# Expert tiles by a transposing DMA: rows scattered as 16-bit planes to a region per expert, in a transformer block with linear attention and a mixture of experts

## The reference, cut to what matters

```python
x = x + attn(layernorm(x))
xf = layernorm(x)                                     # 2048 x 512
scores = xf @ gate_w.T + gate_b + bias                # 2048 x 8
top_scores, top_idx = top_k(scores, 2)
gates = softmax(top_scores)
comb = sum(one_hot(top_idx, 8) * gates[..., None], 1)
h = silu(einsum('td,ehd->teh', xf, w1) + b1)          # hidden size 352
y = einsum('teh,edh->ted', h, w2) + b2
x = x + einsum('ted,te->td', y, comb)
```

## Time and profile before

| | |
|---|---|
| median of three runs | 1009.66 us (1009.46 to 1010.25) |
| the profiled execution | span 1008.9 us from first to last instruction; its own time outside the span is not listed |
| PE busy | 995.8 us, 99% of the span |
| DVE, ACT, POOL busy | 688.1, 513.2, 255.7 us (68%, 51%, 25%) |
| DMA moved | 75.35 MB, mean 75 GB/s |

### The profile page before, as it was taken

One profiled execution on the slowest core, in us unless ns is written; L12 is line 12 of the kernel. 1 busy time (PEld: TensorE's weight loads), 2 busy tenths in 40 slices (PEclk: granted clock), 3 DMA queues, 4 the chain that ended last, 5 costly groups with the idle time before them and its releaser, 6 DMA issues.

```text
span 1008.9 us, 17463 instructions
## 1 busy us (share of the span) xinstructions
PE 995.8 (99%) x5019; PEld 839.2 (83%) x5020; DVE 688.1 (68%) x1554; ACT 513.2 (51%) x1322; POOL 255.7 (25%) x413
## 2 busy tenths in 40 slices
PE   8999999999999999999999999999999989999998
PEld 7888888888888888888788888888888879989996
DVE  6888655665666677767878778887888764544544
ACT  5444444444444447755556555555554954343442
POOL 1000000000000002222433232333333555555554
PEclk9999999999999999999999999999999999999999
DMA  7002501000000012343211121111125645555653
GB/s 263 13 30 84 209 22 40 23 21 21 21 22 21 21 63 63 105 172 116 44 44 51 42 52 42 42 42 42 42 66 149 203 123 102 107 102 101 107 108 48
DMA packets 46862, 75.35 MB, mean 75 GB/s; under 512 B 6090, under 2 KB 18555, under 8 KB 46691
## 3 DMA queue, kind: packets, MB, share of 16 engines
q1 hardware_dynamic: 37010, 56.04, 18.3%
q0 software_dynamic: 9808, 18.79, 10.2%
HBM read 53.14 MB, written 23.50 MB: 76 GB/s over the span
## 4 chain that ended last, share of the span: by engine, by line
PE 93%; DVE 3%; ACT 1%; DMA 1%; issue 1%; SPq 0%; POOL 0%; POOLq 0%; DVEq 0%; ACTq 0%
PE pK L1627 16%; PE pK L1629 16%; PE pK L1628 16%; PE pA L1627 6%; PE pA L1629 6%; PE pA L1628 6%; PE pX L1627 6%; PE pX L1629 5%; PE pX L1628 5%; PE pA L1761 3%; PE pT L1970 2%; PE pT L1707 2%; PE pX L1988 1%; PE pA L1895 1%; PE pK L1895 1%; DMA xn<-in_attn_hidden_states 1%
## 5 line engine op out<-in xcount | busy, mean ns | idle before, releaser
L973 ACT ACTIVATE qs<-q,nrec 128x64 f32<-128x64 f32 x512 | 129.6, 336 | 88.1 <-DVE nrec L1357 85.7
L594 POOL TENSOR_TENSOR wv_lo<-wv_in,wv_hi 128x512 fp32r<-128x512 f32 x4 | 5.2, 1296 | 403.5 <-ACT wo_hi L894 403.5
L1627 PE MATMUL pA<-k_hi,xn_hi 128*128 128x512 f32 x256 | 100.9, 394 | 0.6 <-DVE k_lo L1232 0.6
L1627 PE MATMUL pK<-wk_hi,xnT_hi 128*128 128x512 f32 (+1 forms) x256 | 100.1, 391 | 0.4 <-DVE wk_lo L1212 0.3
L1627 PE MATMUL pK<-wq_hi,xnT_hi 128*128 128x512 f32 x256 | 100.4, 392 | 0.0
L1629 PE MATMUL pK<-wq_hi,xnT_lo 128*128 128x512 f32 x256 | 99.9, 390 | 0.0
L1629 PE MATMUL pA<-k_hi,xn_lo 128*128 128x512 f32 x256 | 99.8, 390 | 0.0
L1628 PE MATMUL pK<-wk_lo,xnT_hi 128*128 128x512 f32 (+1 forms) x256 | 99.7, 390 | 0.0
L1628 PE MATMUL pA<-k_lo,xn_hi 128*128 128x512 f32 x256 | 99.7, 389 | 0.0
L1629 PE MATMUL pK<-wk_hi,xnT_lo 128*128 128x512 f32 (+1 forms) x256 | 99.7, 389 | 0.0
L1628 PE MATMUL pK<-wq_lo,xnT_hi 128*128 128x512 f32 x256 | 99.7, 389 | 0.0
(11 more groups left out here) (291 smaller groups left out, 2446.8 us busy)
## 6 DMA issues: line engine op xcount, KB each, us to landing
w_in<-in_ffn_w SPq DMA_DIRECT2D x22, 256.0 KB, 4.2
w_in<-in_ffn_w SPq DMA_DIRECT2D x8, 704.0 KB, 5.8
xn<-in_attn_hidden_states SPq DMA_DIRECT2D x16, 256.0 KB, 6.2
wv_in<-in_attn_Wv SPq DMA_DIRECT2D x16, 256.0 KB, 2.8
wo_in<-in_attn_Wo SPq DMA_DIRECT2D x16, 256.0 KB, 3.0
wk_in<-in_attn_Wq SPq DMA_DIRECT2D x4, 1024.0 KB, 5.7
xnT_dram<-xnT SPq DMA_DIRECT2D x4, 1024.0 KB, 11.5
x_in<-in_attn_hidden_states SPq DMA_DIRECT2D x16, 256.0 KB, 2.7
```

Source lines behind the costliest of these rows:

```text
L973: i = nc.scalar.activation(qs[:, s], q[:, s], ACT.Copy, scale=nrec[:, b * HC + h:b * HC + h + 1])
L1627: nc.tensor.matmul(dst, lhs[0], rhs[0], start=start, stop=False)
```

## The change

The normalized rows no longer go to DRAM in token order. POOL splits each tile of `xn2` into two planes of 16-bit halves (`put_planes`, a copy of 128 x 1024 uint16), and scatters the 2 KB rows twice by slot (`put_rows`), to `xr_dram`, which is laid out as `meta_dram` is: 17 x 128 rows per expert. An expert tile is then 128 consecutive rows of `xr_dram`; SP loads it with one transposing DMA (128 rows x 1024 halves) into `xgT`, two buffers, at a row number it reads from `meta_row`. ACT joins the low halves into `gx` (`act_rec`), DVE the high halves (`dve_rec`); `gT_hi` and `gT_lo` are then made from `gx` in SBUF. The four PE transposes of each tile and POOL's gathers are gone. Since unused slots must hold numbers, all of `xr_dram` (8 x 2176 rows and 128 more, of 2 KB) is zeroed in the first stage, by DMAs from a 1 KB row of zeros that is repeated. To make room, `gprod` has one buffer instead of two (each dot product waits for the one before), `hT` moves to PSUM, and tiles 0 and 1 have no second set of buffers. The scatters of the last two tiles stand around the gather of the meta rows.

```diff
 [SP]
-            for c in range(1, NC):
-                sp.wait_ge(wk_lo_ready, c * FB)
-                load_wk(c)
+            def zero_rows(first, last):
+                for e in range(first, last):
+                    sp.dma_start(xr_dram[e * EROWS * P:(e + 1) * EROWS * P, :].rearrange("(p r) (h n) -> p (r h) n", p=P, h=2),
+                                 zero16[:, :].unsqueeze(1).to_broadcast([P, 2 * EROWS, D])).then_inc(xr_zeroed, 16)
+
+            sp.wait_ge(wk_lo_ready, FB)
+            load_wk(1)
+            sp.wait_ge(zero_early, 1)
+            zero_rows(0, 3)
+            sp.wait_ge(wk_lo_ready, 2 * FB)
+            load_wk(2)
+            zero_rows(3, 6)
+            sp.dma_start(xr_dram[E * EROWS * P:MROWS * P, :].rearrange("p (h n) -> p h n", h=2),
+                         zero16[:, :].unsqueeze(1).to_broadcast([P, 2, D])).then_inc(xr_zeroed, 16)
+            sp.wait_ge(wk_lo_ready, 3 * FB)
+            load_wk(3)
...
+            zero_rows(6, E)
+            sp.wait_ge(xr_zeroed, 16 * (E + 1))
...
-                sp.wait_ge(xn2_ready, t)
-                sp.dma_start(xn2_dram[ds((t - 1) * P, P), :], xn2[:, :]).then_inc(xn2_stored, 16)
...
+            def load_tile(i):
+                if i >= 2:
+                    sp.wait_ge(rec_lo, i - 1)
+                    sp.wait_ge(rec_hi, i - 1)
+                row = sp.value_load(meta_row[i:i + 1, 0:1], min_val=0, max_val=MROWS - 1)
+                sp.dma_start_transpose(xgT[i % 2][:, :].rearrange("p (c n) -> p c n", n=P),
+                                       xr_dram[ds(row * P, P), :]).then_inc(s_xt[i % 2], 16)
+
+            sp.wait_ge(experts_ready, 1)
+            sp.wait_ge(s_xr, 32 * (NT - 1))
+            sp.wait_ge(s_xr_last, 32)
+            for i in range(NS):
+                load_tile(i)
 [POOL]
+            def put_rows(r, b):
+                rows = xp_last if isinstance(r, int) and r == NT - 1 else xp
+                pool.wait_ge(xp_ready, r + 1)
+                pool.nop(nofuse=True)
+                for c in range(2):
+                    pool.indirect_dma_start(xr_dram, bass.IndirectOffsetOnAxis(slot_i[b][:, c:c + 1].bitcast(U32), 0),
+                                            rows[:, :], None).then_inc(s_xr_last if rows is xp_last else s_xr, 16)
...
+            def put_planes(t):
+                last = isinstance(t, int) and t == NT - 1
+                pool.wait_ge(xn2_ready, t + 1)
+                if not (isinstance(t, int) and t == 0 or last):
+                    pool.wait_ge(s_xr, 32 * t)
...
+                pool.tensor_copy(planes(xp_last if last else xp), words(xn2)).then_inc(xp_ready, 1)
...
             with pool.Fori(2, NT // 2) as h:
                 for b in range(2):
+                    put_planes(2 * h + (b - 2))
                     put_mask(2 * h + (b - 2), b, 32 * h - 32)
                     put_xb(2 * h + b)
                     put_slots(2 * h + (b - 2), b)
...
-            def gather(i):
...
+            put_rows(NT - 2, 0)
             for b in range(2):
                 pool.wait_ge(s_meta[b], 16 * NT)
             pool.indirect_dma_start(meta_in[:, :], None, meta_rows, bass.IndirectOffsetOnAxis(meta_row[:, :].bitcast(U32), 0)
                                     ).then_inc(s_metain, 16)
+            put_rows(NT - 1, 1)
 [ACT]
+            def act_rec(i, b):
+                act.wait_ge(s_xt[b], 16 * (i // 2) + 16 if isinstance(i, int) else 8 * i + (16 - 8 * b))
...
+                    act.wait_ge(gT_lo_ready, i)
+                nc.scalar.copy(words(gx)[:, 0, :], planes(xgT[b])[:, 0, :]).then_inc(rec_lo, 1)
...
-                nc.scalar.copy(g_of(i)[0][:, :], g_bank(i)).then_inc(gT_hi_ready, 1)
+                nc.scalar.copy(gT_hi[:, :], gx[:, :]).then_inc(gT_hi_ready, 1)
 [DVE]
-                        dve.wait_ge(dots_done, E * t + (e - 1 - E))
+                        dve.wait_ge(dots_done, E * t + (e - E))
...
+            def dve_rec(i, b):
...
+                    dve.wait_ge(gT_lo_ready, i)
+                v.tensor_copy(words(gx)[:, 1, :], planes(xgT[b])[:, 1, :]).then_inc(rec_hi, 1)
...
             with dve.Fori(2, NS // 2) as h:
                 for b in range(2):
+                    dve_rec(2 * h + (b + 1), 1 - b)
                     dve_gT(2 * h + (b + 1))
                     dve_y(2 * h + (b - 2), b, 16 * h - 16)
                     dve_hT(2 * h + b, b)
 [PE]
                     i = 2 * h + b
                     pe_h(i, expert(i))
-                    pe_gT(2 * h + (b + 1), 1 - b)
                     pe_y(2 * h + (b - 2), b, expert(2 * h + (b - 2)))
                     pe_hT(i)
```

More of the change, by code:

```diff
@@ L29 @@
 I32 = mybir.dt.int32
+U16 = mybir.dt.uint16
 U32 = mybir.dt.uint32
@@ L215, in block_kernel @@
     gT_lo = sb("gT_lo", D, 186 * KB, F32R)
[L216 to L222, removed]
+    gx = sb("gx", D, 188 * KB)
+    h_in = sb("h_in", H, 190 * KB)
+    hT_hi = [sb("hT_hi0", HB * P, 190 * KB + 1408, F32R), sb("hT_hi1", HB * P, M0 + 5120, F32R)]
+    hT_lo = [sb("hT_lo0", HB * P, 190 * KB + 2944, F32R), sb("hT_lo1", HB * P, 190 * KB + 4480, F32R)]
+    xgT = [sb(f"xgT{b}", 2 * D, (196 + 2 * b) * KB, U16) for b in range(2)]
     y_last = sb("y_last", D, 198 * KB)
@@ L353, in block_kernel @@
         hT_ones = sem("hT_ones")
-        s_g = [sem(f"s_g{i}") for i in range(2)]
+        s_xt = [sem(f"s_xt{i}") for i in range(2)]
+        rec_lo = sem("rec_lo")
+        rec_hi = sem("rec_hi")
         s_add = [sem(f"s_add{i}") for i in range(2)]
-        gT_put = sem("gT_put")
         gT_hi_ready = sem("gT_hi_ready")
@@ L403, in block_kernel @@
         y_bank = lambda i: pA[:, (i - (NS - 2)) * 512:(i - (NS - 3)) * 512] if isinstance(i, int) and i >= NS - 2 else pK[:, 512:1024]
[L406 to L410, removed]
+        hT = pT[:, 0:HB * P]
+        planes = lambda a: a[:, :].rearrange("p (h n) -> p h n", h=2)
+        words = lambda a: a[:, :].bitcast(U16).rearrange("p (n h) -> p h n", h=2)
         @block.sync
@@ L1963, in _ @@
                     meta_transpose()
-            def pe_gT(i, b):
-                pe.wait_ge(s_g[b], 16 * (i // 2) + 16 if isinstance(i, int) else 8 * i + (16 - 8 * b))
-                if not (isinstance(i, int) and i < 2):
-                    pe.wait_ge(gT_lo_ready, i)
-                for n in range(FB):
-                    last = nc.tensor.transpose(g_bank(i)[:, n * P:(n + 1) * P], xg[:, b * D + n * P:b * D + (n + 1) * P], ident[:, :])
-                last.then_inc(gT_put, 1)
             def pe_h(i, e):
                 pe.wait_ge(gT_lo_ready, i + 1)
-                if not (isinstance(i, int) and i < 2):
+                if not (isinstance(i, int) and i < 1):
                     pe.wait_ge(h_ready, i)
                 for n in range(FB):
-                    last = three(h_bank(i), two(g_of(i), n * P, P), two((w1_hi, w1_lo), e * H + n * EH, H),
+                    last = three(pK[:, 0:H], two((gT_hi, gT_lo), n * P, P), two((w1_hi, w1_lo), e * H + n * EH, H),
                                  n == 0, n == FB - 1)
@@ L1987, in pe_hT @@
                     w = min(P, H - n * P)
-                    last = nc.tensor.transpose(hT_bank(i)[0:w, n * P:(n + 1) * P], h_in[:, n * P:n * P + w], ident[:, :])
+                    last = nc.tensor.transpose(pX[0:w, n * P:(n + 1) * P], h_in[:, n * P:n * P + w], ident[:, :])
                 last.then_inc(hT_put, 1)
```

132 lines of the change are left out of this document (69 added, 63 removed).

## The result

The changed kernel takes 1029.6 us (median of 4 runs, 1028.7 to 1030.3), the kernel before 1009.6 beside it: ratio 1.020, 95% interval 1.019 to 1.021. The forecast was 1006.3 in a range of 996 to 1027.

The account below looks back on a forecast made before the run. PE was taken as the bound, busy 99% of the span. From 1009.66 us: loop -14.0, start of the loop +4.6, zeroing +4.5, query stage +1.5, giving 1006.3 us, range 996 to 1027.

Parts of the forecast that it names:

- Zeroing: First stage: zeros queued ahead of load_wk(3) make that load late, and PE stands 4.5 us.
- L: First stage: the time at which load_wk(3) is seen, 98.9 us; PE's stall is worked out from it.
- My line through 2 KB and 1.4 KB pieces: Zeroing: rate for 1 KB pieces from the rates 408 and 396 GB/s, giving 379; 375 was taken.
- Rival C: First stage: zeroing is the stage's bound; break-even is a 7.9 us stall, 1018.7 us at 320 GB/s; chance 0.19.
- Query stage: Query stage: POOL's plane copy meeting qs costs PE 0.1 us per tile, 1.5 us in all; ends 0 and 14.
- The plane copy's 2 us: Query stage: POOL's copy of 1024 elements per tile takes 2 us, between 1.3 and 3.
- the serial dots cost nothing: Query stage: DVE's serial dot products add 0.9 us per token tile, into existing gaps, so they cost nothing.
- Start of the loop: Start of the expert loop: added scatters and the first load behind POOL's table delay h(2) by 4.6 us.
- Loop: Expert loop: period falls from 4.78 to 4.39 us, set by a two-tile chain of 8.79 us; 14.0 us gained over 36 tiles.
- Rival D: Expert loop: the transposing DMA cannot keep the pace; at a period of 6.2 us the time is 1071; chance 0.13.
- B: First stage: zeroing is hidden since 1 KB pieces move at 400 GB/s or more; 1000.3 us, down to 996.4; chance 0.22.
- E: Expert loop: the DVE chain is as long as what it replaces, period 4.78; nothing gained, 1020 us; chance 0.04.

Follow-up runs that it names:

- Experiment 4: Changed kernel with the seven early zeroings written from a 2 KB instead of a 1 KB source row, same places: 1022.9 us, ratio 1.012.
- experiment 5: Changed kernel with GpSimd's plane copy waiting until the eight dots of its tile are done: 1023.65 us, ratio 1.014.
- experiment 7: Changed kernel with VectorE's join of tile i+2 moved right behind gT_lo of tile i+1, ahead of y and hT: 1023.5 us, ratio 1.014.
- experiment 10: Changed kernel with portioned zeroing, reordered query stage, earlier join, and tile 0 loaded early into its own buffer: 1001.2 us; with the meta gather also moved, 1005.6.
- experiment 8: Changed kernel with a plain load of each expert tile instead of the transposing one, tiles left untransposed: 1027.35 us, ratio 1.017.

## Why the prediction was wrong, step by step

- **Zeroing, +4.5 forecast, +14.1 measured: the step that failed.** The stall was L + 3.0 - 97.4, with L = 98.9 from a rate of 375 GB/s. L was 106.5, and the rule gives 12.1. The rate was the mistake: the windows read 384 down to 300, with 319 where a weight load is mixed in; 29.1 MB between 20.6 and 105.3 us are 344 GB/s. A part of that is not the rate of the zeros: all queues moved 30.07 MB in that time, 355 GB/s, and the sum for L had left out the pair loads that SyncE issues from 97.53 us on, right behind load_wk(3), and that share the engines with it. My line through 2 KB and 1.4 KB pieces had the right sign, and the other line (361, from the 512 B row) was nearer. Experiment 4 shows that the size of the piece is a real term, but with it the mean from 20.6 us on is 390 GB/s and not 408: the windows in which weight loads are mixed in stay lower (357 GB/s with load_wk(2), 325 from 90 to 95 us). The last 2 us are those in which PE runs at the 1.2 GHz level after its idle stretch (12 matmuls in 4.48 us instead of 2.72, so 1.8 us); I had no term for that. In experiment 4 the same holds (99.4 + 3.0 - 97.4 = 5.0 by the rule, 6.9 measured, 395.7 - 388.8; the same 12 matmuls take 4.45 us there). The clock's part is read from the starts and was not isolated by a run.
- **Rival C** had this mechanism and a chance of 0.19. At 344 GB/s its own sum, 27.0/344 + 5.1 + 21.8 = 105.4, is right about the load within 1.1 us, and its time would have been 1013: most of the rest of the miss is not in the first stage.
- **Query stage, +1.5 forecast, +9.6 measured.** The plane copy's 2 us was too dear (it takes 1.04), and the slack was read at the wrong instruction. I placed the copy against qs, and VectorE meets it one instruction sooner, in the dot with gw_late. The Trainium skill (SBUF — State Buffer, Who interferes with whom) has the rule that was named in the forecast, and the trace agrees: 2.21 us instead of 0.69 with the copy beside it, 0.69 without (experiment 5). It holds the other way too, since the copy takes 1.48 us when the qs starts first. On who waits the trace does not bear the page out: the page has the order of issue decide it, but the dot starts 0.60 us before the copy (636.01 and 636.61) and is the one that is held, by more than the copy's length; here the measurement decides. I took 0.1 us per tile out of ends of 0 and 1; measured are about 0.5 in each of the nine later periods (4.3 us). The 2.7 us at the rank matmul of tile 1 come from GpSimd's hand-written order in the first two tiles, through which I had not followed the two new scatters and the copy; the fall of the clock behind it (1.6 us in this profile, none in that of experiment 7) had no term either. That the serial dots cost nothing was right.
- **Start of the loop, +4.6 to h(2).** Measured +4.1 to the first h_in; h(2) starts at 851.97, 29.1 us after the earlier trace rows, of which 23.7 were lost before: +5.4. About 1 us of it is the clock: the first h starts at 842.80, +3.1, and takes 1.0 us longer than before, at a mean granted clock of 0.61. The sum was near, but what ends last is not the first load behind GpSimd's table, as I had it: also in the changed kernel ScalarE's joining copy starts at 840.16 straight behind the split of the weights, and in experiment 10 the load goes 2 us sooner and h does not start sooner.
- **Loop, -14.0 forecast, -10.4 measured** for the 36 tiles, 4.49 us each against 4.39. The chain was right to 0.19 us in 8.8. In the period shown, the term that was off is the joining copy: 0.72 for 0.55. Over the loop it is not so simple: between 860 and 1000 us the copy takes 0.45 to 0.50 in 19 of 31 tiles and 0.68 to 0.72 in 12, 0.56 in the mean, as forecast; behind a tile with a long copy the next h follows in 4.53 us in the mean, behind one with a short copy in 4.46, and why also these are above 4.39 is not shown. The 12 long copies start 0.60 to 0.63 us after GpSimd has begun to issue a scatter, as 908.23 behind 907.63 above. Moving the copy out of the chain (experiment 7) gives 0.46 in every tile and a period of 4.38, so the chain through the copy did hold the loop.
- **Rival D is refuted.** The transposing load keeps a pace of 4.38 us in experiment 7, and experiment 8 shows that it costs the loop nothing. The Trainium skill (VectorE: DVE Perf Modes, The three transpose paths) has 1309 ns for a 128 x 128 block; eight blocks come in at most 4.38 us here, 0.55 us each, so the measurement decides against using that figure for a large transposing load. **B** fell with the rate, **E** with the period.
- The forecast said that it is wrong if the stalls exceed the 9.4 us that loop and start leave. They are 23.7 us (14.1 and 9.6), and loop and start leave only 4.9 (9.0 less 4.1): the difference is the 18.8 us.

## What to carry to other kernels

Bulk traffic that nobody waits for still has a place in the order of the engine that issues it: count both the queue in front of the next wanted load and the time for which the issuing engine is held, and put it in portions behind loads that recur, one for each interval that can hold it. A stall can cost more than its length, when the clock falls behind it. A copy moved to an idle engine is free only if the instruction beside it, not the one next after it, can bear the shared port; and an order written out by hand for the first and last tiles must be walked through on its own. When a large change loses, its parts may still be good: with three small reorderings and a second buffer for the planes the same change is 0.7 to 0.8% faster than the kernel before.

## What the runs showed of the hardware that was not expected

- A DMA issue on SyncE takes 0.4 to 0.6 us into an empty queue, also for a region of 4.3 MB. Behind others it is held: 12.4 us in the median of the eight regions of the changed kernel, 15.8 at most (30.00 us for three in a row, of which the first takes little; 62.93 for six), and 12.19 us for 0.26 MB behind six regions.
- Writes to DRAM from a broadcast source run at 384 and 353 GB/s with 1 KB pieces and 408 and 401 with 2 KB pieces, in the same two windows (30 to 40 and 80 to 90 us).
- A VectorE dot with two SBUF inputs beside a GpSimd copy of 1.04 us takes 2.21 us (2.19 to 2.21 in 10 tiles), more than the two one behind the other (1.73), though it starts 0.6 us before the copy.
- Behind the same stall of PE the clock may fall or not: after 2.73 us at the rank matmul the granted clock from 501 to 507 us is 0.72 in the changed kernel's profile and 1.00 in that of experiment 7.
- A VectorE copy between SBUF buffers takes 0.46 us, and 0.68 to 0.72 when it starts 0.60 to 0.63 us into GpSimd's issue of an indirect DMA (1.55 us long). At 0.19 and 0.32 us into it, or at 0.82, it takes 0.45, 0.46 and 0.50. No experiment isolated this.
